# Turning quantised weights behind a mixture of experts, and a gather that is added part by part

## The chip, the cores and the metric

The kernel runs as one program on one core of a Trainium2 chip. The metric is the device time of the whole program in microseconds (us); less is better. Five engines work side by side: TensorE (PE, matmuls and transposes), VectorE (DVE), ScalarE (ACT), GpSimd (POOL, which here also issues the indirect DMAs) and SyncE (SP, which issues the plain DMAs). Each engine runs its own list of instructions in the order in which the program was written, and waits on semaphores that the others raise.

## The reference, cut to what matters

Two decoder layers work on x of shape 32 x 256 x 256 (32 items of 256 tokens of 256 features). The change lies at the seam between the experts that end the first layer and the attention that begins the second.

```
# end of layer 0: one expert for each token, 16 experts of 512 places, hidden size 1024
h = relu(einsum('ecd,edh->ech', buf, W1) + b1);  y = einsum('ech,ehd->ecd', h, W2) + b2
x = x + where(keep, y[idx, safe_pos] * gate, 0)
# start of layer 1: attention over the 32 items of each token position
n = layernorm(x);  q = n @ Wq.T;  k = n @ Wk.T
x = x + softmax(tanh(scores(q, k) / 16), over items) @ n
...
# end of layer 1: a gated feed-forward whose three matrices (w_gate, w_up: 704x256, w_down: 256x704)
# are quantised to FP4 in blocks of 16 along the last dimension; the matmuls need them transposed
gate = xq @ q(w_gate).T;  up = xq @ q(w_up).T;  out = hq @ q(w_down).T
```

## The kernel before, in words

The program is four phases written one behind the other, each closed by an all-engine barrier: phase A (rotary and cross attention of layer 0 with the router), phase C (the experts), phase D (the attention over the items), phase E (cross attention of layer 1 and the quantised feed-forward). Queues within a phase are written out by hand: phase C as a loop over the experts, phases D and E by tables of slots, where `due(n, period, slots, items)` says which step of which item stands at place n of an engine's list.

**Phase C.** For each of 16 experts e, `pe_phase_c` writes on PE: eight up groups (`pe_c_up`, 2 matmuls of 512 columns each into banks 0 to 3), the transposes of the next expert's tokens (`pe_c_turn`, banks 6 and 7), for e = 4 to 14 one step of `pe_weights` (the transposes of a piece of a quantised matrix, 11 steps in all, `TURNS`), and four down groups (`pe_c_down`, 8 matmuls each, banks 4 and 5). `pe_weights` uses bank 6 or 7, and so waits for ACT to have copied the next expert's tokens out of that bank (`act_c_x_t`); `act_weights` then copies the piece into `ff_wg`, `ff_wu` or `ff_wd`, which are read in phase E only. The quantising itself (`dve_weights`, 30 steps on DVE) stands beside experts 1 to 4. `sp_c_out` stores each expert's answer into the DRAM tensor `expert_out`; behind the last one SP waits until all stores have landed (`y_out`), and then the barrier of line 1853 follows.

**Phase D.** 16 steps t, each of G = 4 parts g of 128 rows. POOL gathers the rows of `expert_out` that belong to the step's tokens (`pool_d_gather`, four indirect DMAs, one for each part, into `sa_y`). DVE waits for all four, multiplies by the gate and adds x (`dve_d_add`, four instructions), makes the layer norm's moments (`dve_d_moments`: four BN_STATS, four aggregates, one addition); POOL raises the variance to -1/2 (`pool_d_power`); DVE normalises (`dve_d_normed`); PE transposes (`pe_d_turn`), projects (`pe_d_project`), makes the scores (`pe_d_score`) and, after tanh, exp and a mask, the sums (`pe_d_sum`). DVE adds the sums to x (`dve_d_out`), SP stores them and then loads the x, slots and gates of four steps on. x, slots and gates of steps 0 to 3 are loaded during phase C.

The order of POOL's list in phase D is that of the table: gather at place 2 + 2t, power at place 5 + 2t. So the gather of step 1 (place 4) stands ahead of the power of step 0 (place 5), the gather of step 2 (place 6) behind it. `pool_d_gather` waits for the step's x, slots and gates, and for the add of step t - 2, whose `sa_y` buffer it takes.

Of the kernel before, what the change touches and what calls it, by code (L numbers as in the profile page):

```python
# [11 lines left out]
ALU = mybir.AluOpType  # L12
# [11 lines left out]
KC = D // P  # L24
# [39 lines left out]
class Core:  # L64
# [13 lines left out]
        self.steps = {self.pool_made.name: 0, self.dve_made.name: 0, self.pe_made.name: 0}  # L78
        self.end_phase()

    def end_phase(self):
        self.idle_sems += reversed(self.phase_sems)
        self.phase_sems = []

        self.bank_out = [(self.idle, 0)] * 8

        self.p_out = [(self.idle, 0)] * 8

# [36 lines left out]
    return t - lag if 0 <= t - lag < n else None  # L125


def due(n, period, slots, items=B):

    for k, slot in enumerate(slots):  # L130
        b, off = divmod(n - slot, period)
        if off == 0 and 0 <= b < items:
            yield b, k


# [1360 lines left out]

FC = -(-FI // P)  # L1500
WIDTHS = [min(P, FI - k * P) for k in range(FC)]
HALF = FI // 2
# [283 lines left out]
def pe_phase_c(c):  # L1786
    for k in range(KC):
        pe_c_turn(c, 0, k)
    for e in range(E):
        for m1 in range(MC):  # L1790
            pe_c_up(c, e, m1)
        if e + 1 < E:
            for k in range(KC):
                pe_c_turn(c, e + 1, k)
        if e == 3:
            pe_positions(c)
        if 4 <= e < 4 + TURNS:
            pe_weights(c, e - 4)
        for q in range(QC):
            pe_c_down(c, e, q)  # L1800


def act_phase_c(c):
    for k in range(KC):
        act_c_x_t(c, 0, k)
    for e in range(E):
        for m1 in range(0, MC, 2):
            act_c_hidden(c, e, m1)
        if e + 1 < E:
            for k in range(KC):  # L1810
                act_c_x_t(c, e + 1, k)
        if e == 3:
            act_positions(c)
        if 4 <= e < 4 + TURNS:
            act_weights(c, e - 4)


def dve_phase_c(c):
# [27 lines left out]
def phase_c(c, d):  # L1846
    setup_c(c)
    raw_weights(c)
    sp_phase_c(c, d)
    pe_phase_c(c)  # L1850
    act_phase_c(c)
    dve_phase_c(c)
    c.nc.all_engine_barrier()  # L1853

# [51 lines left out]
def setup_d(c):  # L1908
    nc, r, s = c.nc, c.sa, c.sa.s
    r.y, r.x3 = c.ring("sa_y", 2, [P, G, D]), c.ring("sa_x3", 4, [P, G, D])  # L1910
    r.out, r.xn = c.ring("sa_out", 2, [P, G, D]), c.ring("sa_xn", 4, [P, G, D + 1])
    r.xn_t, r.q = c.ring("sa_xnt", 2, [P, KC, G * P]), c.ring("sa_q", 2, [P, KC, G * P])
    r.weight, r.rec = c.ring("sa_p", 2, [P, G, P]), c.sb("sa_rec", [P, G])
    r.stats, r.mv = c.sb("sa_stats", [P, G, 6]), c.sb("sa_mv", [P, G, 2])
    r.var, r.rstd = c.sb("sa_var", [P, G]), c.sb("sa_rstd", [P, G])
    n = STEPS_D
    s.y_in = [c.new_sem(f"sa_y_in{i}") for i in range(2)]
    s.x3, s.ln, s.pow = c.sem("sa_x3", n), c.sem("sa_ln", 4 * n), c.sem("sa_pow", n)
    s.turned, s.xn_t = c.sem("sa_xnT", 2 * n), c.sem("sa_xnt", 2 * n)
    s.projected, s.q = c.sem("sa_proj", 2 * n), c.sem("sa_q", 2 * n)  # L1920
    s.scored, s.tanh, s.exp, s.weight = (c.sem("sa_" + name, n) for name in ("score", "tanh", "exp", "w"))
    s.summed, s.rec, s.out, s.out_there = c.sem("sa_pv", 4 * n), c.sem("sa_rec", 4 * n), c.sem("sa_done", 4 * n), c.pair("sa_out_there", 16 * n // 2)
    for ring in range(4):
        c.step(c.dve_made, nc.vector.memset(r.xn[ring][:, :, D:D + 1], 1.0))
    c.dve.wait_ge(*c.all_of(c.dve_made))
    c.dve.wait_ge(s.same, 1)
    c.pe.wait_ge(s.both, 1)
# [25 lines left out]
def pool_d_gather(c, answer, t):  # L1953
    s, r, par = c.sa.s, c.sa, t % 2
    c.pool.wait_ge(s.x_in[t % 4], 48 * (t // 4 + 1))
    c.pool.wait_ge(s.x3, t - 1)
    for g in range(G):
        c.nc.gpsimd.indirect_dma_start(  # L1958
            r.y[par][:, g, :], None, answer, bass.IndirectOffsetOnAxis(ap=r.slot[t % 4][:, g:g + 1], axis=0),
            bounds_check=answer.shape[0] - 1, oob_is_err=False).then_inc(s.y_in[par], 16)  # L1960


def dve_d_add(c, t):

    s, r, dve, par, at = c.sa.s, c.sa, c.nc.vector, t % 2, t % 4
    c.dve.wait_ge(s.x_in[at], 48 * (t // 4 + 1))
    c.dve.wait_ge(s.y_in[par], 64 * (t // 2 + 1))
    c.dve.wait_ge(s.out, 4 * (t - 3))
    for g in range(G):
        m = dve.scalar_tensor_tensor(out=r.x3[at][:, g, :], in0=r.y[par][:, g, :], scalar=r.gate[at][:, g:g + 1],  # L1970
                                     in1=r.x[at][:, g, :], op0=ALU.mult, op1=ALU.add)
    m.then_inc(s.x3, 1)


def dve_d_moments(c, t):
    s, r, dve, at = c.sa.s, c.sa, c.nc.vector, t % 4
    c.dve.wait_ge(s.x3, t + 1)
    for g in range(G):
        m = dve.bn_stats(r.stats[:, g, :], r.x3[at][:, g, :])
    m.then_inc(s.ln, 1)  # L1980
# [624 lines left out]
def build(nc, d):  # L2605
# [5 lines left out]
    with ExitStack() as ctx:  # L2611
# [5 lines left out]
        for phase in (phase_a, phase_c, phase_d, phase_e):  # L2617
# [51 lines left out]
```

## Time and profile before

| | us |
|---|---|
| median of three runs | 3308.53 |
| the runs | 3308.53, 3306.96, 3313.92 |
| profiled execution, device time | 3310.97 |
| profiled execution, span from the first to the last instruction | 3309.2 |
| of it PE busy | 3089.0 (93%) |
| DVE busy | 2335.3 (71%) |
| ACT busy | 1786.9 (54%) |
| POOL busy | 1278.0 (39%) |
| mean granted TensorE clock | 0.971 |

All times within the trace are us from the span's start. The phases' borders in it: phase A to about 1380, phase C to about 1856, phase D to about 2025, phase E to the end. Of the 1.8 us between the span and the device time of the same execution nothing is in the trace. A row of the timeline gives start, duration, engine, line, operation, the tiles written and read, how many instructions it merges (x), and in brackets how long the engine sat idle before it and what ended that. Matmul ends are modelled, so a following row may begin a little before the one above it ends.

### The profile page before, as it was taken

What the parts mean: (1) busy time and instruction counts of PE and PEld (TensorE: products, weight loads), DVE (VectorE), ACT (ScalarE), POOL (GpSimd) and SP (SyncE); (2) the same over time, 40 slices, a digit from 0 to 9 for tenths busy, and PEclk for the clock granted to TensorE, in tenths of its full rate; (3) what the DMA queues carried; (4) which work ended last, traced back from release to release, by engine and by line L of the source; (5) the groups of instructions that cost most, each with busy time, mean ns of one, the idle gap of its engine ahead of it and who ended that gap; (6) DMA issues with size and microseconds to landing.
All of it is one profiled execution on the core that took longest, in us unless ns stands there. A gap on an engine that the chain in (4) does not pass through costs nothing. (4 is left out here: it accounts for less than half of the span.)

```text
span 3309.2 us, 57683 instructions
## 1 busy us (share of the span) xinstructions
PE 3089.0 (93%) x21302; PEld 2142.9 (65%) x21302; DVE 2335.3 (71%) x4796; ACT 1786.9 (54%) x3245; POOL 1278.0 (39%) x1929
## 2 busy tenths in 40 slices
PE   3799999999999998699999796899999999999998
PEld 2566666666666665366666454567777777777765
DVE  4588888888888887242111385587788877888786
ACT  3788888888888874211111132455555555555553
POOL 4366666666666663100000361133333333333321
PEclk8999999999999998799999897899999999999999
DMA  5887788887788882333234253433344333433330
GB/s 108 140 129 102 110 111 111 114 114 102 106 110 111 111 102 44 124 119 114 96 109 145 64 172 94 72 57 57 62 72 64 59 57 62 71 63 61 57 49 14
DMA packets 291117, 301.17 MB, mean 91 GB/s; under 512 B 35258, under 2 KB 278442, under 8 KB 290836
## 3 DMA queue, kind: packets, MB, share of 16 engines
q1 hardware_dynamic: 276436, 273.41, 48.9%
q0 software_dynamic: 6144, 15.68, 1.9%
q10 hardware_dynamic: 8256, 8.39, 0.8%
q8 instruction: 169, 2.77, 0.4%
q14 instruction: 112, 0.92, 0.1%
HBM read 95.51 MB, written 50.40 MB: 44 GB/s over the span
## 5 line engine op out<-in xcount | busy, mean ns | idle before, releaser
L493 DVE TENSOR_REDUCE xa_mx<-bank 128x2 f32<-128x512 f32 x1024 | 664.2, 687 | 257.8 <-PE bank L483 251.0
L597 ACT ACTIVATE xa_p<-bank 128x512 f32<-128x512 f32 x1024 | 566.3, 598 | 294.0 <-PE bank L587 270.9
L608 DVE SCALAR_TENSOR_TENSOR xa_p<-xa_p,bank 128x1024 f32<-128x1024 f32 x256 | 303.6, 1217 | 30.0 <-ACT xa_p L597 22.9
L620 PE MATMUL bank<-xa_p,xa_v 128*32 128x256 f32 x4096 | 278.6, 390 | 0.5 <-DVE xa_p L608 0.3
L1958 POOL DMA_INDIRECT sa_y<-expert_out,sa_s x64 | 70.6, 1103 | 522.6 <-POOLq L1853 483.4
L933 POOL TENSOR_SCALAR_AFFINE_SELECT xa_p<-xa_p 128x256 f32<-128x256 f32 x512 | 197.0, 407 | 174.9 <-ACT xa_p L924 174.7
L924 ACT ACTIVATE xa_p<-bank 128x384 f32<-128x384 f32 x512 | 231.0, 495 | 51.3 <-PE bank L912 39.9
L1747 ACT ACTIVATE ex_h<-bank,ex_b 128x512 f32<-128x512 f32 x64 | 44.0, 687 | 362.4 <-PE bank L1736 362.4
L1736 PE MATMUL bank<-ex_xt,ex_w 128*128 128x512 f32 x512 | 225.2, 598 | 0.7 <-ACT ex_xt L1727 0.7
L1766 PE MATMUL bank<-ex_w,ex_h 128*128 128x256 f32 x1024 | 224.0, 379 | 1.0 <-issue 0.9
L1766 PEld LDWEIGHTS bank<-ex_w,ex_h 128*128 128x128 f32 x1024 | 193.4, 190 | 28.1 <-issue 2.4
L587 PE MATMUL bank<-xa_qs,xa_ks 99*128 99x256 bf16 x1024 | 185.5, 277 | 13.9 <-DMA xa_qs<-xa_row 5.3
L483 PE MATMUL bank<-xa_ks,xa_qs 96*128 96x256 bf16 x1024 | 187.4, 277 | 8.4 <-DVE xa_mx L493 5.9
L2294 ACT ACTIVATE fe_g<-bank 128x352 f32<-128x352 f32 x128 | 59.1, 462 | 241.3 <-PE bank L2276 240.8
L483 PE MATMUL bank<-xa_ks,ex_w 96*128 96x256 bf16 x1024 | 174.3, 277 | 15.5 <-DMA ex_w<-xa_pq 10.4
L1551 POOL TENSOR_TENSOR fp_v<-fp_v,fp_p 128x1408 f32<-128x1408 f32 x31 | 98.5, 3179 | 230.2 <-DVE fp_v L1542 230.2
L587 PE MATMUL bank<-ex_w,xa_ks 99*128 99x256 bf16 x1024 | 170.3, 277 | 10.5 <-DMA ex_w<-xa_row 7.8
L454 PE MATMUL bank<-ff_wd,fe_ht 128*128 128x256 f32 x744 | 168.9, 383 | 7.4 <-ACT fe_ht L1651 6.1
L2276 PE MATMUL bank<-ff_wg,fe_xnt 128*128 128x352 f32 x512 | 172.8, 460 | 3.0 <-DVE ex_w L2310 1.6
L1736 PEld LDWEIGHTS bank<-ex_xt,ex_w 128*128 128x128 f32 x512 | 98.3, 192 | 118.3 <-issue 116.5
L1776 DVE TENSOR_TENSOR ex_y<-bank,ex_b 128x256 f32<-128x256 f32 x64 | 27.2, 425 | 203.6 <-PE bank L1766 203.6
L620 PEld LDWEIGHTS bank<-xa_p,xa_v 128*32 128x32 f32 x4096 | 107.9, 110 | 94.8 <-issue 49.4
(294 smaller groups left out, 6933.5 us busy)
## 6 DMA issues: line engine op xcount, KB each, us to landing
ex_w<-ra_parts SPq DMA_DIRECT2D x384, 128.0 KB, 7.0
xa_ks<-xa_pk SPq DMA_DIRECT2D x384, 128.0 KB, 5.4
ex_w<-in_L_ffn_W SPq DMA_DIRECT2D x32, 1024.0 KB, 7.1
xa_qs<-xa_pq SPq DMA_DIRECT2D x192, 128.0 KB, 4.7
ex_w<-xa_pq SPq DMA_DIRECT2D x192, 128.0 KB, 4.5
ra_x<-in_x SPq DMA_DIRECT2D x32, 256.0 KB
xa_ctx<-in_ctx_t SPq DMA_DIRECT2D x64, 128.0 KB
queue<-zeros ACTq DMA_DIRECT2D x4, 2048.0 KB, 14.0
```

Source lines behind the costliest of these rows:

```text
L454: m = c.nc.tensor.matmul(ps[:, tc * D:(tc + 1) * D], left[:, k, tc * P:(tc + 1) * P], right[:, k, :], start=(k == 0), stop=(k == chunks - 1))
L483: m = c.nc.tensor.matmul(ps[:, tc * S:(tc + 1) * S], c.xa.q_stack[par][0:STACK3, h, tc * P:(tc + 1) * P], c.xa.k_stack[par][0:STACK3, h, : ...
L493: c.nc.vector.tensor_reduce(c.xa.row_max[:, :, n], halves(c.banks[2 + n % 2]), AX.X, ALU.max).then_inc(s.max_taken, 1)
L587: m = c.nc.tensor.matmul(ps[:, kc * S:(kc + 1) * S], c.xa.k_stack[par][:, h, kc * P:(kc + 1) * P], c.xa.q_stack[par][:, h, :], start=True, ...
L597: c.nc.scalar.activation(c.xa.p_beside[:, n // 2 % 4, :, n % 2, :], halves(c.banks[n % 2]), ACT.Exp, scale=SCALE).then_inc(s.exp, 1)
L608: c.nc.vector.scalar_tensor_tensor(out=p, in0=p, scalar=1.0, in1=c.banks[bank][:, :].unsqueeze(1).broadcast_to([P, TC, 2 * S]), op0=ALU.mi ...
L620: m = c.nc.tensor.matmul(bank[WIDE * quad:WIDE * quad + WIDE, at + q0:at + S], v[:, kc, 4 * g + quad, :], p(4 * g + quad, kc), start=(kc = ...
L924: c.nc.scalar.activation(c.xa.p_after[:, n // 2 % 4, n % 2, 0:S + P], c.banks[n % 2][:, 0:S + P], ACT.Exp, scale=1.0 / math.sqrt(2.0 * DH) ...
L933: c.nc.gpsimd.affine_select(out=diagonal, in_=diagonal, compare_op=ALU.is_ge, fill=0.0, base=0, pattern=[[0, TC], [1, P]], channel_multipl ...
L1736: m = c.nc.tensor.matmul(c.banks[bank][:, :], r.w1[par][:, k, m1 * P:(m1 + 1) * P], r.x_t[par][:, k, :], start=(k == 0), stop=(k == KC - 1))
L1766: m = c.nc.tensor.matmul(c.banks[bank][:, 0:D], r.hid[par][:, k, q * P:(q + 1) * P], r.w2[par][:, k, :], start=(k == 0), stop=(k == MC - 1))
L2276: m = c.nc.tensor.matmul(c.banks[bank][:, 0:HALF], c.ff.xn_t[:, k, tc * P:(tc + 1) * P], w[:, k, cols], start=(k == 0), stop=(k == KC - 1))
```

## The change

1. The 11 steps of `pe_weights` and `act_weights` leave the loop over the experts and stand behind it, on PE and on ACT, one after the other.
2. The barrier between phases C and D is gone. In its place POOL waits for the stores of `expert_out`. SP's own wait for them stays. `end_phase` keeps what banks 6 and 7 wait for, so that phase D's first transposes wait for ACT's last copies; some tiles of phase D are declared in another order.
3. Step 0 of phase D gets a function of its own, `dve_d_first`: each of the four gathers raises its own semaphore, and DVE adds a part and takes its BN_STATS as soon as that part is there. Its aggregates follow.
4. On POOL the gather and the power of step 0 are written ahead of the table, which begins with step 1.

The parts of the diff that matter:

```diff
@@ pe_phase_c @@
-        if 4 <= e < 4 + TURNS:
-            pe_weights(c, e - 4)
         for q in range(QC):
             pe_c_down(c, e, q)
+    for n in range(TURNS):
+        pe_weights(c, n)
@@ act_phase_c @@
-        if 4 <= e < 4 + TURNS:
-            act_weights(c, e - 4)
+    for n in range(TURNS):
+        act_weights(c, n)
@@ phase_c @@
-    c.nc.all_engine_barrier()
+    for out in c.ex.s.y_out:
+        c.pool.wait_ge(out, 16 * (E // 2))
@@ pool_d_gather @@
-            bounds_check=answer.shape[0] - 1, oob_is_err=False).then_inc(s.y_in[par], 16)
+            bounds_check=answer.shape[0] - 1, oob_is_err=False).then_inc(s.y_in[par] if t else s.y_first[g], 16)
@@ new @@
+def dve_d_first(c):
+    s, r, dve = c.sa.s, c.sa, c.nc.vector
+    c.dve.wait_ge(s.x_in[0], 48)
+    for g in range(G):
+        c.dve.wait_ge(s.y_first[g], 16)
+        m = dve.scalar_tensor_tensor(out=r.x3[0][:, g, :], in0=r.y[0][:, g, :], scalar=r.gate[0][:, g:g + 1],
+                                     in1=r.x[0][:, g, :], op0=ALU.mult, op1=ALU.add)
+        done = (s.x3_first, g + 1) if g < G - 1 else (s.x3, 1)
+        m.then_inc(done[0], 1)
+        c.dve.wait_ge(*done)
+        m = dve.bn_stats(r.stats[:, g, :], r.x3[0][:, g, :])
+    m.then_inc(s.ln, 1)
+    dve_d_moments(c, 0)
@@ dve_phase_d @@
+    dve_d_first(c)
...
-        for b, _ in due(n, period, (16,), STEPS_D):
+        for b, _ in due(n, period, (16,), STEPS_D, first=1):
@@ pool_phase_d @@
+    pool_d_gather(c, d["expert_out"], 0)
+    pool_d_power(c, 0)
...
-        for b, _ in due(n, period, (2,), STEPS_D):
+        for b, _ in due(n, period, (2,), STEPS_D, first=1):
             pool_d_gather(c, d["expert_out"], b)
-        for b, _ in due(n, period, (5,), STEPS_D):
+        for b, _ in due(n, period, (5,), STEPS_D, first=1):
             pool_d_power(c, b)
```

TensorE's list before, from the last expert with a weight step to phase D's first transposes (`raw_down` is the quantised w_down, `ex_x` an expert's tokens, `ex_h` its hidden values, `sa_xn` phase D's normalised rows):

```order
L1736 MATMUL bank<-ex_xt,ex_w 128x512 x16
L1718 MATMUL bank<-ident,ex_x 128x128 x8
L304 MATMUL bank<-ident,raw_down 128x128 x2
L304 MATMUL bank<-ident,raw_down 64x128 x2
L1766 MATMUL bank<-ex_w,ex_h 128x256 x32
L1736 MATMUL bank<-ex_xt,ex_w 128x512 x16
L1766 MATMUL bank<-ex_w,ex_h 128x256 x32
L2011 MATMUL bank<-ident,sa_xn 128x128 x8
```

And the same place now (lines are those of the changed file):

```order
L1738 MATMUL bank<-ex_xt,ex_w 128x512 x16
L1720 MATMUL bank<-ident,ex_x 128x128 x8
L1768 MATMUL bank<-ex_w,ex_h 128x256 x32
L1738 MATMUL bank<-ex_xt,ex_w 128x512 x16
L1768 MATMUL bank<-ex_w,ex_h 128x256 x32
L1626 MATMUL bank<-ident,raw_gate 128x128 x12
L1626 MATMUL bank<-ident,raw_up 128x128 x12
L306 MATMUL bank<-ident,raw_down 128x128 x10
L306 MATMUL bank<-ident,raw_down 64x128 x2
L2033 MATMUL bank<-ident,sa_xn 128x128 x8
```

All 36 transposes of matrices now stand in one row between the last expert's down matmuls and phase D's first transposes.

POOL's list before, at the start of phase D (the number behind `sa_y` is the buffer, that behind `sa_s` the ring place of the step's slots, 0 to 3 for steps 0 to 3):

```order
L1958 DMA sa_y0<-expert_out,sa_s0 128x256 x4
L1958 DMA sa_y1<-expert_out,sa_s1 128x256 x4
L1993 TENSOR_TENSOR sa_rstd<-sa_var,mhalf 128x4
L1958 DMA sa_y0<-expert_out,sa_s2 128x256 x4
L1993 TENSOR_TENSOR sa_rstd<-sa_var,mhalf 128x4
```

And now:

```order
L1963 DMA sa_y0<-expert_out,sa_s0 128x256 x4
L2015 TENSOR_TENSOR sa_rstd<-sa_var,mhalf 128x4
L1963 DMA sa_y1<-expert_out,sa_s1 128x256 x4
L1963 DMA sa_y0<-expert_out,sa_s2 128x256 x4
L2015 TENSOR_TENSOR sa_rstd<-sa_var,mhalf 128x4
```

The gather of step 1 has moved from ahead of the power of step 0 to behind it, and stands together with the gather of step 2. From the power of step 1 on the two lists are alike.

## Rows read from the trace of the kernel before

**Rows 1.** Windows by phase, C and D: busy us, (x instructions), clock, DMA, GB/s

```profile
core 0: us, PE busy (x) PEld busy (x) DVE busy (x) ACT busy (x) POOL busy (x), PEclk, DMA share, GB/s
...
1380.00:1856.00 476.00, 468.47 (x1710) 312.36 (x1710) 106.80 (x157) 67.87 (x110) 0.00 (x0) 0.99 0.35 115
1856.00:2025.30 169.30, 138.20 (x641) 88.67 (x640) 125.89 (x419) 54.50 (x96) 87.16 (x80) 0.93 0.43 137
```

**Rows 2.** Timeline of PE in phase C: start, duration, what

```profile
1414.24 13.90 PE L1736 MATMUL bank<-ex_xt,ex_w 128*128 128x512 f32 x32
...
1442.92 13.90 PE L1736 MATMUL bank<-ex_xt,ex_w 128*128 128x512 f32 x32
...
1502.81 13.90 PE L1736 MATMUL bank<-ex_xt,ex_w 128*128 128x512 f32 x32
1516.54 1.04 PE L1718 MATMUL bank<-ident,ex_x 128*128 128x128 f32 x8
1517.92 0.63 PE L1624 MATMUL bank<-ident,raw_gate 128*128 128x128 f32 x4 [0.34 <-ACT ex_xt L1727]
...
1827.18 13.90 PE L1736 MATMUL bank<-ex_xt,ex_w 128*128 128x512 f32 x32
```

**Rows 3.** ACT's copies of turned weights (line 1638): ns min/median/max

```profile
L1638 ACT ACTIVATE ff_wg<-bank x4: 330/464/597, 1518.6 to 1607.1; 128x512 f32<-128x512 f32 x2, 128x192 f32<-128x192 f32 x2
```

**Rows 4.** The barrier (line 1853) on SP's queue: ns, and start in us

```profile
L1853 SPq DRAIN  x1: 7/7/7, 1859.5 to 1859.5; - x1
...
L1853 SPq EVENT_SEMAPHORE  x1: 17/17/17, 1859.7 to 1859.7; - x1
```

**Rows 5.** Timeline of POOL at the start of phase D

```profile
1860.54 1.06 POOL L1958 DMA_INDIRECT sa_y<-expert_out,sa_s  x1 [483.43 <-POOLq L1853]
...
1864.52 1.00 POOL L1958 DMA_INDIRECT sa_y<-expert_out,sa_s  x1 [0.31 <-issue]
1865.82 1.00 POOL L1958 DMA_INDIRECT sa_y<-expert_out,sa_s  x1 [0.30 <-issue]
...
1869.88 0.99 POOL L1958 DMA_INDIRECT sa_y<-expert_out,sa_s  x1 [0.30 <-issue]
1871.25 1.04 POOL L1993 TENSOR_TENSOR sa_rstd<-sa_var,mhalf 128x4 f32<-128x4 f32 x1 [0.37 <-DVE sa_mv L1983]
1872.48 1.20 POOL L1958 DMA_INDIRECT sa_y<-expert_out,sa_s  x1 [0.19 <-issue]
...
1876.74 1.01 POOL L1958 DMA_INDIRECT sa_y<-expert_out,sa_s  x1 [0.30 <-issue]
```

**Rows 6.** Timeline of DVE at the start of phase D

```profile
1867.43 1.67 DVE L1970 SCALAR_TENSOR_TENSOR sa_x<-sa_y,sa_g,sa_x 128x256 f32<-128x256 f32 x4 [7.44 <-DMA sa_y<-expert_out,sa_s]
1869.13 1.41 DVE L1979 BATCH_NORM_STATS2 sa_stats<-sa_x 128x6 f32<-128x256 f32 x4
...
1872.33 1.44 DVE L2001 TENSOR_SCALAR sa_xn<-sa_x,sa_mv,sa_rstd 128x256 f32<-128x256 f32 x4 [1.17 <-POOL sa_rstd L1993]
1874.27 1.67 DVE L1970 SCALAR_TENSOR_TENSOR sa_x<-sa_y,sa_g,sa_x 128x256 f32<-128x256 f32 x4 [0.50 <-DMA sa_y<-expert_out,sa_s]
...
1879.17 1.44 DVE L2001 TENSOR_SCALAR sa_xn<-sa_x,sa_mv,sa_rstd 128x256 f32<-128x256 f32 x4 [1.16 <-POOL sa_rstd L1993]
```

**Rows 7.** Timeline of PE in phase D: steps 0 and 1, and the transposes of step 15

```profile
1873.82 1.97 PE L2011 MATMUL bank<-ident,sa_xn 128*128 128x128 f32 x8 [17.80 <-DVE sa_xn L2001]
...
1882.48 2.05 PE L2048 MATMUL bank<-sa_q,sa_xnt 128*128 128x128 f32 x16 [0.69 <-ACT sa_q L2039]
1884.37 1.04 PE L2011 MATMUL bank<-ident,sa_xn 128*128 128x128 f32 x8
...
2011.05 1.09 PE L2011 MATMUL bank<-ident,sa_xn 128*128 128x128 f32 x8 [0.22 <-DVE sa_xn L2001]
```

**Rows 8.** Window of the 6 us behind PE's restart (columns as in Rows 1)

```profile
1873.80:1879.80 6.00, 5.29 (x12) 3.07 (x13) 4.26 (x15) 1.19 (x2) 4.67 (x5) 0.50 0.32 90
```

**Rows 9.** Waits in phase D, one group: us in total, times, longest us

```profile
POOL sa_y L1958 <- DMA sa_g<-gates: 23.7, 11, 3.2
```

**Rows 10.** Timeline of POOL in phase D, the longest of the 64 gather instructions

```profile
1950.76 1.90 POOL L1958 DMA_INDIRECT sa_y<-expert_out,sa_s  x1 [0.30 <-issue]
```

More of the change, by code:

```diff
@@ L79, in __init__, with end_phase @@
         self.end_phase()
-    def end_phase(self):
+    def end_phase(self, banks=()):
         self.idle_sems += reversed(self.phase_sems)
         self.phase_sems = []
-        self.bank_out = [(self.idle, 0)] * 8
+        self.bank_out = [self.bank_out[i] if i in banks else (self.idle, 0) for i in range(8)]
         self.p_out = [(self.idle, 0)] * 8
@@ L125, in item, with due @@
     return t - lag if 0 <= t - lag < n else None
-def due(n, period, slots, items=B):
+def due(n, period, slots, items=B, first=0):
     for k, slot in enumerate(slots):
         b, off = divmod(n - slot, period)
-        if off == 0 and 0 <= b < items:
+        if off == 0 and first <= b < items:
             yield b, k
@@ L1579, in raw_weights @@
     s.loaded, s.quant = c.sem("weights_in", 16 * 11), c.sem("weights_fp4", 30)
-    s.turned, s.copied = c.sem("weightsT", TURNS), c.sem("weights_t", TURNS)
+    s.turned, s.copied = c.sem("weightsT"), c.sem("weights_t")
     for raw in f.raw[0:2]:
@@ L1910, in setup_d @@
     r.y, r.x3 = c.ring("sa_y", 2, [P, G, D]), c.ring("sa_x3", 4, [P, G, D])
[L1911 to L1914, printed above, removed]
+    r.xn, r.xn_t = c.ring("sa_xn", 4, [P, G, D + 1]), c.ring("sa_xnt", 2, [P, KC, G * P])
+    r.stats, r.mv, r.rec = c.sb("sa_stats", [P, G, 6]), c.sb("sa_mv", [P, G, 2]), c.sb("sa_rec", [P, G])
     r.var, r.rstd = c.sb("sa_var", [P, G]), c.sb("sa_rstd", [P, G])
+    r.q, r.out, r.weight = c.ring("sa_q", 2, [P, KC, G * P]), c.ring("sa_out", 2, [P, G, D]), c.ring("sa_p", 2, [P, G, P])
     n = STEPS_D
-    s.y_in = [c.new_sem(f"sa_y_in{i}") for i in range(2)]
+    s.y_in, s.y_first = [c.new_sem(f"sa_y_in{i}") for i in range(2)], [c.new_sem(f"sa_y_first{g}") for g in range(G)]
+    s.x3_first = c.sem("sa_x3_first")
     s.x3, s.ln, s.pow = c.sem("sa_x3", n), c.sem("sa_ln", 4 * n), c.sem("sa_pow", n)
@@ L1966, in dve_d_add @@
     c.dve.wait_ge(s.x_in[at], 48 * (t // 4 + 1))
-    c.dve.wait_ge(s.y_in[par], 64 * (t // 2 + 1))
+    c.dve.wait_ge(s.y_in[par], 64 * (t // 2 + par))
     c.dve.wait_ge(s.out, 4 * (t - 3))
@@ L1972, in dve_d_add @@
     m.then_inc(s.x3, 1)
+def dve_d_first(c):
[11 more added lines that the diff above has]
+    dve_d_moments(c, 0)
 def dve_d_moments(c, t):
     s, r, dve, at = c.sa.s, c.sa, c.nc.vector, t % 4
[L1977 to L1980, printed above, removed]
+    if t:
+        c.dve.wait_ge(s.x3, t + 1)
+        for g in range(G):
+            m = dve.bn_stats(r.stats[:, g, :], r.x3[at][:, g, :])
+        m.then_inc(s.ln, 1)
     c.dve.wait_ge(s.ln, 4 * t + 1)
@@ L2120, in dve_phase_d @@
 def dve_phase_d(c):
+    dve_d_first(c)
     period = ROUND_D["dve"]
     for n in range((STEPS_D - 1) * period + 40):
-        for b, _ in due(n, period, (16,), STEPS_D):
+        for b, _ in due(n, period, (16,), STEPS_D, first=1):
             dve_d_add(c, b)
-        for b, _ in due(n, period, (18,), STEPS_D):
+        for b, _ in due(n, period, (18,), STEPS_D, first=1):
             dve_d_moments(c, b)
@@ L2623, in build @@
                 phase(c, d)
-            c.end_phase()
+            c.end_phase((6, 7) if phase is phase_c else ())
 def kernel(**inputs):
```

## The prediction

> **What bounds the kernel now.** First the windows by phase [rows 1]. In phase C PE is busy 468.5 of 476 us, at full clock: the experts are bound by PE, DVE and ACT are mostly idle and POOL does nothing. So there a microsecond that leaves PE's path is a microsecond of the kernel. Phase D (169.3 us) has PE at 138.2 and DVE at 125.9, and its start is a hole: PE's last down matmul ends at 1856.0, its next work begins at 1873.82 after 17.8 us idle [rows 7]. That hole is a chain: store of the last expert, barrier, four gathers, add, moments, power, normalise, transposes. Next I read PE's timeline in phase C for what a round (one expert) takes with and without a weight step, then POOL, DVE and PE at the seam in that order, since the chain goes from one to the next. Phase E stands behind a barrier of its own and is not touched; it moves as a block.
>
> **Turns leave the rounds.** A round without a turn takes 1442.92 - 1414.24 = 28.68 us [rows 2]. That round has quantising steps on DVE beside it and is no slower for it. The eleven rounds with a turn run from 1502.81 to 1827.18, 324.37 us [rows 2], or 29.49 each. Eleven plain rounds would take 11 x 28.68 = 315.48. The difference is **8.9 us**. Its make-up is seen in the first of them: the token transposes start at 1516.54 and the turn only at 1517.92 after a wait of 0.34 us for ACT's copy of those tokens out of the bank, so one pays for a bank wait as well as for the transposes. All of it lies on PE's path, with the hidden values ready: nothing else is late in the plain rounds. I see no reason for the removed turns to leave less than this; what bounds it is that rounds of both kinds are equal to 0.3 us among themselves, so 8.5 to 9.1.
>
> **Turns behind the rounds.** They now run on PE and ACT after the last down matmul. PE's four transposes take 0.63 us [rows 2], ACT's copy 0.33 or 0.60 [rows 3]. Two banks alternate; one bank needs transposes, copy and two hand-overs of some 0.2 to 0.3 us, about 1.6 us for a pair of steps on both banks, so eleven steps take about 5.5 x 1.6 = 9 us, and 11 x (0.63 + 0.60 + 0.5) = 19 us were nothing to overlap. The cover is the hole: 17.8 us before, some 15.3 after the next two terms. I take 0; without any overlap it would be late by 4. For the last expert nothing is queued behind the turns that the chain needs: its answers are added on DVE and stored by SP.
>
> **Barrier.** SP sees the stores landed at 1859.5 and the barrier lets go at 1859.7 [rows 4]; the first gather starts at 1860.54 [rows 5]. POOL now waits for the same stores itself. The 0.2 us go for sure; the 0.84 us between release and gather may be set-up that stays. Bounds 0 to 1.0, I take **0.3**, nearest to the barrier's own rows.
>
> **First residual.** The last of four gathers starts at 1864.52, DVE is released at 1867.43: 2.91 us to landing. The gathers start 1.3 us apart, and one part's add (1.67/4 = 0.42) and statistics (1.41/4 = 0.35) [rows 6] fit between two of them. So behind the last landing stand one add and one statistic (some 0.9 with the extra hand-over) in place of 1.67 + 1.41 = 3.08: **2.2 us** less. With the barrier's 0.3 the power of step 0 moves from 1871.25 to 1868.75 and PE's first transposes from 1873.82 to 1871.3.
>
> [...] What the trace shows: a gather instruction takes 1.0 us, and 1.90 at its longest [rows 10]. [...]
>
> **Where that gain goes.** It reaches the rest only if step 1 comes earlier too, and here the order on POOL counts. Before, step 1's gathers ran at 1865.82 to 1870.9, ahead of power 0, while POOL waited for DVE anyway [rows 5]. Now they stand behind power 0. From the power's start to the first gather behind it are 1872.48 - 1871.25 = 1.23 us, so step 1's first gather starts at 1868.75 + 1.23 = 1869.98, **4.2 us later** than before. The last of the four starts 1876.74 - 1872.48 = 4.26 later, at 1874.24. To landing: 2.91 (step 0), or 1874.27 - 1869.88 = 4.39 (step 1) [rows 5, 6]. The slower one had step 4's load issued right beside it; that load is released by the first add, and so now comes well ahead. I take 2.91: add 1 at 1877.15 (before 1874.27). Then as before: 4.90 us from add to normalise, and 1.49 to the transposes [rows 6, 7]: PE's step 1 at 1883.54, against **1884.37** before, where it only queued behind step 0's scores (1882.48 + 2.05). Those scores now end at 1882.0, so PE idles 1.5 us. Of a head start of 2.5 us **0.8** is left. With the slower landing step 1 comes at 1885.0, 0.7 later than before.
>
> From here the two kernels have the same lists, and PE runs back to back. The gather of step 2 stands ahead of power 1 in both. It would end at about 1880.7, and power 1 is wanted at 1877.15 + 3.82 = 1881.0: just clear. The low clock changes nothing: before, the clock was 0.50 until 6 us after PE's restart [rows 8]. I assume the same again at 1871.3. Were it full, the first transposes and projections would be done earlier, but the transposes of step 1 wait for DVE all the same.
>
> **The sum.** -8.9 (rounds) - 0.8 (what is left at step 1) = **-9.7 us**. The profiled span becomes 3309.2 - 9.7 = 3299.5. That execution took 3310.97, 2.4 above the median of 3308.53; against the median I predict **3298.8 us**. Own range of this case: rounds 8.5 to 9.1, step 1 from -1.9 (barrier 1.0 instead of 0.3, landing half a us quicker) to +0.7, so 3297.5 to 3300.7.
>
> **Rivals.**
> - The head start holds: step 1 is ready when PE is, and 2.5 us reach the end. -8.9 - 2.5: **3297.1**. Against: it needs add 1 at 1875.6, 5.6 us after its first gather, where the two rows show 6.9 and 8.4. Chance 0.10.
> - Late gathers: a slow landing (4.39), or DVE's part-wise adds holding two gathers for 0.42 each, or power 1 held by gather 2. Step 1 comes at 1885 to 1886, phase D starts 0.7 to 1.5 us later than before. -8.9 + 1: **3300.6**. [...] For it: the margin at power 1 is 0.3 us, and gathers up to 1.90 exist. Chance 0.25.
> - The rounds don't get shorter, since something else fills the turn's place (the tokens' copies, the weights' loads). -0.8 alone: **3307.7**, no change. Against: three plain rounds at 28.7. Half of the gain would be 3303. Chance 0.05.
> - Slower: phase D's steady loop slips. Step 1 to step 15 take 2011.05 - 1884.37 = 126.7 us, 9.05 each [rows 7], and POOL waits in 11 steps for the gates' load, 23.7 us in all [rows 9], with the power of the step before queued behind that gather. If the shifted start left the load of every step about 0.7 us later against its gather, the power would be late by as much each time: 14 x 0.7 = 9.8, just the gain. From 0.7 us a step on the kernel is slower; at 1.2, 3308.5 - 9.7 + 16.8 = **3315.6**. Against: the load follows the step's own output, so loop and load shift together. Chance 0.03.
>
> **How the numbers follow.** Forecast 0.57, the rivals 0.10, 0.25, 0.05, 0.03. Median to median, a measurement of this kernel can tell about 0.2% (6.6 us) from no change; the three runs alone spread from 3306.96 to 3313.92. Faster by over 0.2% means below 3301.9: forecast, head start, and nearly all of the late gathers, 0.91. Within 0.2%: 0.06. Slower: 0.03. The range takes in the head start, the late gathers, and some 1.5 us for the medians: 3295.5 to 3302.5.
>
> **What would show it.** Rounds 4 to 14 of phase C at 28.7 us each. 36 transposes of matrices behind the last down matmul, done before phase D's first transposes. Four adds in four separate places on DVE, with only one behind the last landing. Step 1's gathers behind power 0, and PE idle for about 1.5 us ahead of its transposes, whose distance from the last expert's down matmuls (1856.0 to 1884.37, 28.4 us) falls by only 0.8. The prediction is wrong if this distance falls by 2 or more (head start), if it grows, or if the rounds keep more than 0.3 us of the turns.

## The result and the profile after

| | before | changed kernel |
|---|---|---|
| median | 3310.22 us (10 runs) | 3302.21 us (10 runs) |
| spread of the runs | 3304.76 to 3313.92 | 3297.49 to 3306.20 |
| profiled execution, device time | 3310.97 us | 3298.72 us |
| its span | 3309.2 us | 3297.0 us |
| its mean granted TensorE clock | 0.971 | 0.979 |

The ratio of the two is 0.9978, with a 95% interval of 0.9969 to 0.9986: 7.3 us less (4.6 to 10.3); the two medians lie 8.0 apart. The change makes the kernel faster, by somewhat less than the 9.7 us forecast. The two profiled executions differ by more than the medians, 12.2 us (3310.97 to 3298.72), and the first thing to see is where. The timeline of PE in the changed kernel (start, duration, what; `ex_h` hidden values, `raw_...` the quantised matrices, `sa_xn` phase D's normalised rows):

```profile
1379.47 1.97 PE L1720 MATMUL bank<-ident,ex_x 128*128 128x128 f32 x8 [12.79 <-DMA ex_x<-queue]
1382.12 15.66 PE L1738 MATMUL bank<-ex_xt,ex_w 128*128 128x512 f32 x32 [0.69 <-ACT ex_xt L1729]
...
1412.61 13.90 PE L1738 MATMUL bank<-ex_xt,ex_w 128*128 128x512 f32 x32
...
1501.18 13.90 PE L1738 MATMUL bank<-ex_xt,ex_w 128*128 128x512 f32 x32
...
1816.61 13.90 PE L1738 MATMUL bank<-ex_xt,ex_w 128*128 128x512 f32 x32
1831.40 14.05 PE L1768 MATMUL bank<-ex_w,ex_h 128*128 128x256 f32 x64 [0.89 <-issue]
1845.29 0.82 PE L1626 MATMUL bank<-ident,raw_gate 128*128 128x128 f32 x6
...
1852.07 0.66 PE L306 MATMUL bank<-ident,raw_down 128*128 128x128 f32 x4 [0.25 <-ACT ff_wd L1650]
1860.79 1.97 PE L2033 MATMUL bank<-ident,sa_xn 128*128 128x128 f32 x8 [8.07 <-DVE sa_xn L2023]
1863.45 5.34 PE L2051 MATMUL bank<-sa_xnt,sa_wqk 128*128 128x512 f32 x8 [0.69 <-ACT sa_xnt L2043]
1869.48 2.05 PE L2070 MATMUL bank<-sa_q,sa_xnt 128*128 128x128 f32 x16 [0.69 <-ACT sa_q L2061]
1873.18 1.09 PE L2033 MATMUL bank<-ident,sa_xn 128*128 128x128 f32 x8 [1.65 <-DVE sa_xn L2023]
```

These rows answer to [rows 2, 7]. The eleven rounds run from 1501.18 to 1816.61, 315.43 us for 324.37: **8.94** less. From the last down matmul's end (1831.40 + 14.05 = 1845.45) to step 1's transposes (1873.18) are 27.73 us for 28.35: **0.62** less. Together 9.56. The other 2.6 us lie where nothing was changed: phase C begins 0.5 earlier, its first round (1382.12 to 1412.61, 30.49 for 31.59 us) is 1.1 shorter, since the granted clock rose earlier (1.00 from 1385.5 on, where before it was still 0.50 at 1387.5), and what follows step 1, phase E with it, is 1.0 shorter.

Here are POOL and DVE at the seam, the place where phase C ends and phase D begins; they answer to [rows 5, 6]. First POOL:

```profile
1849.75 1.06 POOL L1963 DMA_INDIRECT sa_y<-expert_out,sa_s  x1 [474.05 <-DMA expert_out<-ex_y]
...
1853.73 1.00 POOL L1963 DMA_INDIRECT sa_y<-expert_out,sa_s  x1 [0.31 <-issue]
1858.22 1.04 POOL L2015 TENSOR_TENSOR sa_rstd<-sa_var,mhalf 128x4 f32<-128x4 f32 x1 [3.49 <-DVE sa_var L2009]
1859.45 1.20 POOL L1963 DMA_INDIRECT sa_y<-expert_out,sa_s  x1 [0.19 <-issue]
...
1863.59 1.01 POOL L1963 DMA_INDIRECT sa_y<-expert_out,sa_s  x1 [0.30 <-issue]
```

Then DVE:

```profile
1852.71 0.48 DVE L1986 SCALAR_TENSOR_TENSOR sa_x<-sa_y,sa_g,sa_x 128x256 f32<-128x256 f32 x1 [6.75 <-DMA sa_y<-expert_out,sa_s]
...
1856.57 0.48 DVE L1986 SCALAR_TENSOR_TENSOR sa_x<-sa_y,sa_g,sa_x 128x256 f32<-128x256 f32 x1 [0.35 <-DMA sa_y<-expert_out,sa_s]
1857.09 0.43 DVE L1991 BATCH_NORM_STATS2 sa_stats<-sa_x 128x6 f32<-128x256 f32 x1
...
1866.78 1.67 DVE L1975 SCALAR_TENSOR_TENSOR sa_x<-sa_y,sa_g,sa_x 128x256 f32<-128x256 f32 x4 [6.04 <-DMA sa_y<-expert_out,sa_s]
```

POOL's first gather is now let go by the store's landing itself, not by the barrier. The part-wise adds wait for one landing each, and one add stands behind the last. POOL idles 3.49 us ahead of power 0, and step 1's first gather comes at 1859.45 only, 9.70 us behind step 0's first; before, it was 5.28 (1860.54 to 1865.82). DVE then waits 6.04 us for step 1's rows, and PE 1.65 us for DVE. So the fourth of the changes (POOL's new order) takes back most of what the third (the part-wise add) gives.

### The profile page after: what moved, and what is told of

It reads as the page before. It is cut to its first block and busy times, and to the rows that moved or that the text cites. A ratio compares the mean times of both kernels' runs of the same rounds, so it can differ in the third digit from the quotient of the medians.

```text
span 3297.0 us, 57673 instructions
## 1 busy us (share of the span) xinstructions
PE 3088.8 (94%) x21302; PEld 2141.7 (65%) x21302; DVE 2334.7 (71%) x4796; ACT 1786.0 (54%) x3245; POOL 1277.9 (39%) x1929
## 5 line engine op out<-in xcount | busy, mean ns | idle before, releaser
L610 DVE SCALAR_TENSOR_TENSOR xa_p<-xa_p,bank 128x1024 f32<-128x1024 f32 x256 | 303.4, 1215 | 30.2 <-ACT xa_p L599 23.2
L485 PE MATMUL bank<-xa_ks,ex_w 96*128 96x256 bf16 x1024 | 173.9, 276 | 15.8 <-DMA ex_w<-xa_pq 12.1
L2301 PE MATMUL bank<-ff_wu,fe_xnt 128*128 128x352 f32 x512 | 167.2, 459 | 0.6 <-ACT fe_g L2319 0.6
```

The source lines that it names most:

```text
L485: m = c.nc.tensor.matmul(ps[:, tc * S:(tc + 1) * S], c.xa.q_stack[par][0:STACK3, h, tc * P:(tc + 1) * P], c.xa.k_stack[par][0:STACK3, h, : ...
L610: c.nc.vector.scalar_tensor_tensor(out=p, in0=p, scalar=1.0, in1=c.banks[bank][:, :].unsqueeze(1).broadcast_to([P, TC, 2 * S]), op0=ALU.mi ...
L2301: m = c.nc.tensor.matmul(c.banks[bank][:, 0:HALF], c.ff.xn_t[:, k, tc * P:(tc + 1) * P], w[:, k, cols], start=(k == 0), stop=(k == KC - 1))
```

## The experiments

One measure serves for all: where things stand in the trace, counted from the end of the last expert's down matmuls. Two traces of the changed kernel agree in it to 0.3 us in the sum, two of the split gather to 0.1 (though two of its terms moved by 0.6 and 0.7, against each other), while the times of whole runs scatter by several us. Everything in a row of the table but the ratio comes from one trace of that kernel; the ratio rests on 5 to 11 runs of it. In the table "rounds" is the time of the eleven rounds of experts 4 to 14, "step 0" and "step 1" are the starts of phase D's first and second transposes, "to 15" the way from step 1's to step 15's transposes, and "path" the sum of the three differences to before (rounds, step 1, to 15). "By ratio" is the ratio to the kernel before, measured beside it, with its 95% interval.

| kernel | rounds | step 0 | step 1 | to 15 | path | by ratio |
|---|---|---|---|---|---|---|
| before | 324.37 | 17.80 | 28.35 | 126.68 | 0 | |
| changed kernel | 315.43 | 15.34 | 27.73 | 126.14 | -10.1 | 0.9978 (0.9969 to 0.9986) |
| after_again | 315.43 | 15.33 | 27.77 | 126.45 | -9.8 | 0.9974 (0.9965 to 0.9983) |
| turns_only | 315.43 | 22.28 | 33.49 | 126.87 | -3.6 | 0.9979 (0.9970 to 0.9988) |
| seam_only | 324.38 | 15.34 | 27.79 | 126.81 | -0.4 | 1.0 (0.999 to 1.001) |
| whole_first | 315.43 | 17.61 | 28.85 | 126.68 | -8.4 | 0.9977 (0.9968 to 0.9986) |
| old_pool_order | 315.43 | 17.14 | 28.38 | 126.34 | -9.3 | 0.9964 (0.9950 to 0.9978) |
| split_gather | 315.43 | 15.32 | 25.84 | 126.89 | -11.2 | 0.9967 (0.9955 to 0.9980) |
| split_again | 315.43 | 15.37 | 26.43 | 126.22 | -11.3 | 0.9965 (0.9951 to 0.9979) |
| warm_only | 315.43 | 22.57 | 30.63 | 127.19 | -6.2 | 0.9986 (0.9977 to 0.9996) |
| split_warm | 315.44 | 22.57 | 30.62 | 126.63 | -6.7 | 0.9980 (0.9970 to 0.9989) |
| warm9_only | 315.44 | 16.10 | 28.25 | 129.04 | -6.7 | 0.9978 (0.9968 to 0.9989) |
| warm9_split | 315.43 | 15.70 | 25.13 | 129.72 | -9.1 | 0.9961 (0.9947 to 0.9974) |
| turns_twice | 315.43 | 15.29 | 27.36 | 129.38 | -7.2 | 0.9973 (0.9962 to 0.9984) |

**The changed kernel again.**

> The changed kernel once more, nothing left out. Question: is the gain 9.6 us (path theory: 8.9 from the eleven rounds, 0.6 from the seam, as the two traces show them) or some 7 to 8 us, as the medians of the runs so far have it (3310.22 and 3302.21)? Path theory: the distance from the last expert's last down matmul to the transposes of step 1 of phase D is 27.7 us again, a round of the experts 28.68, and the medians differ by 9.6, give or take the 2 us by which medians of a kernel wander. Rival (something is given back later, in phase E): the gain stays under 8.0 and phase E is longer than before by 1.5 us or more in this trace too (it was 0.9 longer in the first).

Median 3302.65 us (11 runs) beside 3311.86 (33 runs of before): 9.2 between the medians, 8.6 by the ratio. Taken together, the means of the changed kernel's 21 runs and of the 43 runs of before beside them (3302.3 and 3310.9) lie 8.6 us apart, with a 95% interval of about 7.0 to 10.3, worked out from the scatter of these runs. Rounds and seam are the same to 0.05 us. The rival asked for a longer phase E; from its first matmuls to the end it took 1273.6 us here, 1277.4 in the changed kernel's first trace and 1276.5 in that of before. So no loss of phase E's is tied to the change; phase E wanders by 4 us with the same code in it.

**The turns alone.** The loop edits of the diff (`pe_phase_c`, `act_phase_c`) in the kernel before, nothing else:

> The kernel before with one edit: the eleven weight steps stand behind the loop over the experts on PE and on ACT; the barrier and phase D stay as they were. Path theory: rounds of 28.68 us, 8.9 less in the sum; but the barrier makes PE and ACT drain, and the last copy of weights ends 8.0 us behind the last down matmul (1853.4 against 1845.45 in the changed kernel), while the stores landed after 3.5. So the barrier opens some 4.3 us later than its stores would allow, and of 8.9 only 4.6 are left: median about 3305.6 beside 3310.2. Rival (the barrier costs the turns nothing, since the drain overlaps): the full 8.9, 3301.3.

The barrier on each queue of this kernel (ns, start in us), POOL's first gather behind it, and ACT's last copy of weights:

```profile
L1853 SPq DRAIN  x1: 7/7/7, 1853.0 to 1853.0; - x1
...
L1853 ACTq DRAIN  x1: 672/672/672, 1856.8 to 1856.8; - x1
L1853 SPq EVENT_SEMAPHORE  x1: 17/17/17, 1857.7 to 1857.7; - x1
...
1858.51 1.06 POOL L1958 DMA_INDIRECT sa_y<-expert_out,sa_s  x1 [479.27 <-POOLq L1853]
...
1857.10 0.36 ACT L1651 ACTIVATE ff_wd<-bank 64x256 f32<-64x256 f32 x1
```

SP is ready at 1853.0, the barrier opens at 1857.7, when ACT's last copy is done. The first transposes come 22.28 us behind the last down matmul for 17.80, 4.5 later (4.3 expected), step 1's 5.1 later. So of 8.9 us the barrier takes back 4.5, and a longer low clock in step 0 (projections of 5.99 us for 5.32) another 0.7. In the times this is not as clear: the ratio says 7.0 us (4.0 to 9.9). That interval leaves out the path's 3.6 by a little, and it holds the expected 4.6 as well as the rival's 8.9, and the 8.6 of the changed kernel's second set. The trace shows the mechanism, a first gather held until ACT's last copy; how much of it the whole time feels is not settled by the times.

**The seam alone.** The changed kernel with the weight steps back in the loop over the experts, on PE and on ACT; `end_phase` keeps bank 6 only:

> The changed kernel with the eleven weight steps put back into the rounds of experts 4 to 14, on PE and ACT; the missing barrier, the part-wise first add and POOL's new order stay. Path theory: rounds of 29.5 us as before, first transposes of phase D 2.5 us earlier against the last down matmul than before (15.3 for 17.8 us), transposes of step 1 only 0.6 earlier (27.7 for 28.35): total 0.6 less than before, 3309.6 beside 3310.2, which the times can't tell from no change. Rival (the seam carries more of the gain than its first step shows): 2 us or more less, with step 1 at 26 us or under.

Ratio 1.0 (0.999 to 1.001), step 1 at 27.79. The first transposes come 2.5 us earlier, and nothing of it arrives at step 1 but 0.6. Step 0's projections took 5.95 us here for 5.34 in the changed kernel, and step 1 stands at the same place: PE still idled 1.11 us ahead of it, for DVE. The medians (3308.88 beside 3311.86) lie 3 apart, inside their scatter.

**Without the part-wise add.** The third and fourth change are undone: step 0's gathers raise the table's semaphore again, DVE waits for all four, and POOL has its old order. The parts of the edit that matter:

```diff
-    dve_d_first(c)
...
-    pool_d_gather(c, d["expert_out"], 0)
-    pool_d_power(c, 0)
...
-        for b, _ in due(n, period, (2,), STEPS_D, first=1):
+        for b, _ in due(n, period, (2,), STEPS_D):
```

> The changed kernel without its third and fourth edit: step 0 of phase D waits for all four gathers again and adds them in one go, and POOL has its old order (gather of step 1 ahead of power 0). Turns behind the rounds and no barrier. Path theory: the first transposes come 2.2 us later than in the changed kernel (17.5 us behind the last down matmul for 15.3), but step 1 is ready when PE is, so its transposes stand at 28.1 for 27.7: total only 0.4 more than the changed kernel. Rival (the part-wise add is worth its 2.2 us): 2.2 more than the changed kernel.

Step 0 at 17.61, 2.3 later, and step 1 at 28.85, 1.1 later than the changed kernel where 0.4 was expected. The 0.7 more is PE's clock: step 0's projections took 6.00 us here, 5.34 in the changed kernel. In time it can't be told from the changed kernel (0.9977 and 0.9978). So the third and the fourth change together bring step 1 forward by 1.1 us, 0.7 of it the clock's, and no run shows them in the time.

**POOL's order.** With `pool_d_gather(c, d["expert_out"], 1)` between the gather and the power of step 0, and the table's gathers from step 2 on:

> The changed kernel with one edit: on POOL the four gathers of step 1 stand ahead of power 0 again, as before the change; the part-wise add stays. Order theory: the gathers run while POOL waits for DVE (3.5 us idle) but end 1.7 us behind the moment at which power 0 could start, so the first transposes come about 1.7 later than in the changed kernel (17.0 us behind the last down matmul for 15.3); step 1's add comes some 4 us earlier, and step 1's transposes wait for PE instead of for DVE: 27.5 for 27.7 us. Total the same within 0.2 us. Rival (step 1's gathers were not what held its transposes): step 1's transposes stay behind the first by as much as now, 12.4 us, and come at 29.4.

Step 0 at 17.14 as expected; step 1 at 28.38, not 27.5, again because the projections took 6.01 us at the low clock. The rival (step 1 at 29.4) falls: with the gathers early, step 1's transposes follow step 0's scores without idling. So POOL's order only chooses which of the two waits. Its five runs gave 0.9964, with an interval wide enough to hold the path's 9.3. That ratio is no worse than the split gather's below, though the paths differ by 1.9 us: the times of so few runs don't rank these orders, the traces do.

**Two gathers ahead, two behind.**

```diff
     pool_d_gather(c, d["expert_out"], 0)
+    pool_d_gather(c, d["expert_out"], 1, range(0, 2))
     pool_d_power(c, 0)
+    pool_d_gather(c, d["expert_out"], 1, range(2, G))
...
-        for b, _ in due(n, period, (2,), STEPS_D, first=1):
+        for b, _ in due(n, period, (2,), STEPS_D, first=2):
```

> The changed kernel with one edit: two of the four gathers of step 1 stand ahead of power 0, two behind it. Order theory: two gathers (2.6 us) fit into POOL's 3.5 us of waiting, so power 0 and the first transposes stay where they are (15.3 us behind the last down matmul), the last gather of step 1 lands 2.6 us earlier, and step 1's transposes come when PE is free, 25.9 to 26.0 us for 27.7: 1.8 us less than the changed kernel, and the head start of 2.4 is kept whole against before. Rival (landing slows as gathers come together with step 4's load, or power 0 is pushed): 27 us or more.

POOL's timeline in this kernel, then PE's:

```profile
1857.22 1.00 POOL L1963 DMA_INDIRECT sa_y<-expert_out,sa_s  x1 [0.30 <-issue]
1859.08 1.05 POOL L2015 TENSOR_TENSOR sa_rstd<-sa_var,mhalf 128x4 f32<-128x4 f32 x1 [0.86 <-DVE sa_var L2009]
...
1861.66 1.97 PE L2033 MATMUL bank<-ident,sa_xn 128*128 128x128 f32 x8 [8.04 <-DVE sa_xn L2023]
1864.32 5.29 PE L2051 MATMUL bank<-sa_xnt,sa_wqk 128*128 128x512 f32 x8 [0.69 <-ACT sa_xnt L2043]
1870.29 2.05 PE L2070 MATMUL bank<-sa_q,sa_xnt 128*128 128x128 f32 x16 [0.69 <-ACT sa_q L2061]
1872.18 1.04 PE L2033 MATMUL bank<-ident,sa_xn 128*128 128x128 f32 x8
```

POOL's wait ahead of power 0 shrinks from 3.49 to 0.86 us, power 0 is not pushed, and PE no longer waits for step 1: 25.84 us, 2.5 less than before. This is the whole head start. It was run once more:

> The split gather once more, nothing left out, to see whether it beats both kernels by more than single traces tell. Path theory: 8.9 from the rounds, 2.5 from the seam (step 1's transposes at 25.8 us behind the last down matmul for 28.35 before), so 11.4 less than before, a ratio of 0.9965; a round of 28.68. Rival (the seam's gain is lost again in phase D, as the kernel with 9 unused matmuls lost 3 us there): the way from step 1's to step 15's transposes is 128 us or more for 126.7, and the ratio is 0.9973 as of the changed kernel.

3301.04 us beside 3311.81, ratio 0.9965; step 1 at 26.43, 0.6 above the first time and above the 25.8 expected, and 126.22 us from there to step 15. The 0.6 is the low clock again: step 0's projections took 5.83 us for 5.29, and here PE is what step 1 waits for. Both ratios (0.9967, 0.9965) lie below both of the changed kernel (0.9978, 0.9974), though the intervals overlap. Of all kernels here this one has the longest path gain: 11.2 and 11.3 us for 9.8 to 10.1.

**PE kept busy over the hole.**

```diff
 def pe_phase_d(c):
+    for _ in range(18):
+        c.nc.tensor.matmul(c.banks[0][:, :], c.consts.ident[:, :], c.sa.both[:, :, :], start=True, stop=True)
```

> The changed kernel with 18 matmuls of 512 columns added on PE ahead of phase D, their result not used (computation unchanged otherwise); they fill PE's idle 8 us between the last turned weight and the first transposes. Theory: the granted clock stays at 1.0, so the first transposes take 1.04 for 1.97 us and the first projection 3.70 for 5.34, step 0's scores end 2.5 us earlier; step 1's transposes wait for DVE and stay at 27.7 us, so the total is the same within 0.3 us. Rival (the low clock lies on the path): step 1's transposes come earlier too, by 1 us or more.

> Both edits together: two of step 1's gathers ahead of power 0, and the 18 unused matmuls that fill PE's idle time. Theory: with the split gather step 1's transposes wait for PE, whose first projection ran at the low clock; with the clock at 1.0 they wait for DVE again, at about 25.1 us behind the last down matmul: 0.9 less than the split gather alone, 2.6 less than the changed kernel, so that the clock counts only once the gathers do not hold. Rival: no more than the split gather alone, 25.9.

Both were mis-sized: one such matmul is two rows of 0.43 us in the trace, so 18 last 15.6 us and themselves put step 0 at 22.57, against an expected 15.3; on the path they lost some 4 us against the same kernels without them, and neither answers its rival. They show one thing cleanly: with the granted clock at 1.00, step 1 follows step 0 by 8.06 us, where PE is what binds it (10.5 to 11.2 at the low clock). With 9:

> As the warm_only kernel, with 9 unused matmuls for 18: there each took 0.87 us (two passes of 0.43), so that 18 lasted 15.6 us and pushed the first transposes to 22.6 us; 9 last 7.8 and end ahead of the first transposes. Theory: clock 1.0 throughout, first transposes at 15.3 to 15.5 us behind the last down matmul, step 0's scores done 2.5 us earlier, step 1's transposes where DVE lets them: 27.7 us as in the changed kernel. Rival (the low clock lies on the path of the changed kernel): step 1 at 26.7 or less.

> The split gather (two of step 1's gathers ahead of power 0, two behind) with the 9 unused matmuls. Theory: the clock stays at 1.0 and step 1's transposes wait for DVE again, at about 25.1 us behind the last down matmul, for 25.84 with the split gather alone and 27.73 in the changed kernel; total 2.6 less than the changed kernel. Rival (the split gather's step 1 was held by DVE or the landing, not by PE's low clock): 25.8 again.

PE's timeline in the kernel with 9 unused matmuls and the changed kernel's gathers:

```profile
1867.14 1.09 PE L2033 MATMUL bank<-ident,sa_xn 128*128 128x128 f32 x8 [1.09 <-DVE sa_xn L2023]
1868.97 3.70 PE L2051 MATMUL bank<-sa_xnt,sa_wqk 128*128 128x512 f32 x8 [0.74 <-issue]
1873.36 2.05 PE L2070 MATMUL bank<-sa_q,sa_xnt 128*128 128x128 f32 x16 [0.69 <-ACT sa_q L2061]
1879.29 1.97 PE L2033 MATMUL bank<-ident,sa_xn 128*128 128x128 f32 x8 [3.88 <-DVE sa_xn L2023]
1881.94 5.58 PE L2051 MATMUL bank<-sa_xnt,sa_wqk 128*128 128x512 f32 x8 [0.69 <-ACT sa_xnt L2043]
```

Step 0 runs at full clock (1.09 and 3.70) and starts at 16.10 for the 15.3 to 15.5 expected, since its last gather landed later (3.56 us from its start to the add, 2.84 in the changed kernel); step 1 waits for DVE, as expected, at 28.25 for 27.7. But now PE has 3.88 us of nothing in front of step 1, and the low clock comes there instead. The windows of this kernel (columns as in [rows 1]; the clock is the third number from the end):

```profile
1877.00:1878.00 1.00, 0.00 (x0) 0.00 (x0) 0.21 (x1) 0.00 (x0) 0.81 (x2) 1.00 0.47 131
...
1879.00:1880.00 1.00, 0.71 (x4) 0.72 (x5) 1.00 (x4) 0.00 (x0) 0.69 (x2) 0.50 0.19 37
```

The transposes take 1.97, the projections 5.58, and step 15 comes 129.04 us behind step 1 for 126.1 to 127.2 in all the others but warm9_split and turns_twice, which follow. On the path the low clock's cost was not removed, it was moved to step 1. The time doesn't show the loss: 0.9978, as for the changed kernel. With the split gather step 1 comes at 25.13, as expected, and the clock stays full through its first steps; that trace then lost 3.0 us later, between steps 4 and 6 (10.74 and 9.77 us for two steps of about 9.1) and between steps 7 and 8 (10.48). POOL in it, ahead of step 5:

```profile
1903.70 1.07 POOL L1963 DMA_INDIRECT sa_y<-expert_out,sa_s  x1 [3.60 <-DMA sa_g<-gates]
1905.08 1.83 POOL L1963 DMA_INDIRECT sa_y<-expert_out,sa_s  x1 [0.31 <-issue]
...
1909.57 1.04 POOL L2015 TENSOR_TENSOR sa_rstd<-sa_var,mhalf 128x4 f32<-128x4 f32 x1
```

The gather waited 3.60 us for the gates, one instruction took 1.83 us, and the power stood behind them: the loop of the fourth rival, in single steps. PE idled 2.04 us for it, and the low clock came back for a part of step 5 (0.50 from 1914 to 1916, projections of 4.84 us for 3.70). The trace of warm_only has one such step too, from step 13 to 14 (10.47 us, with a wait of 4.04 us for the gates on POOL); no trace without unused matmuls has one. Whether that is chance is open. The five runs of warm9_split gave the lowest ratio of all, 0.9961, and its interval (8.6 to 17.6 us) holds the trace's 9.1 only at its end, and has the 12.1 that the path would give without the lost steps near its middle: this speaks against a loss in every run.

**The turns twice.** Every weight step behind the rounds made two times:

> The changed kernel with every weight step behind the rounds made twice (22 steps for 11, the same results written again). It measures the cover. Theory: eleven steps took 8.0 us, so 22 end at 15.9 us behind the last down matmul, 0.6 later than the first transposes could start (15.3): these come at 15.5 to 16.2; step 1's transposes wait for DVE and stay at 27.7, so doubling the hidden work costs nothing, and PE's clock stays at 1.0 or falls only after the restart. Rival (the turns are not free: they slow the gathers, the copies or the last answers): step 1 at 28.5 or later, total up by 1 us or more.

Step 0 at 15.29, step 1 at 27.36: the seam doesn't feel eleven more turns, so the cover is real and not used up. Here too PE stayed busy up to step 0, ran it at full clock, and then idled 3.80 us ahead of step 1, and the low clock (0.50; step 1's transposes 1.48 us for 1.09, its projections 6.27 for 3.70) cost 2.7 us behind it (129.38). The expectation had "costs nothing", and its rival had the total up by 1 us or more; step 1 is not later, but the path as a whole is up: 2.9 us more than in the changed kernel. The turns themselves hold nothing up at step 0 or step 1; the loss is the clock's, but the added turns brought it, by moving PE's gap. The time (0.9973) shows no loss beside the changed kernel's 0.9978.

## Why the prediction came out as it did

**Rounds.** 8.9 forecast, 8.94 in every trace of a kernel with the edit. Right.

**Turns behind the rounds.** Some 9 us forecast, 8.0 measured, inside the hole: PE's down matmuls end at 1845.45 and ACT's last copy ends at 1853.41. The hand-overs, estimated at 0.2 to 0.3 us each, lie in this trace within the idle times between one piece and the next, 0.25 to 0.56 us on PE and 0.26 to 0.59 on ACT.

```profile
1853.05 0.36 ACT L1653 ACTIVATE ff_wd<-bank 64x256 f32<-64x256 f32 x1
```

Right; doubling them left step 0 where it was.

**Barrier.** 0.3 forecast: from the last down matmul to the first gather 4.30 us for 4.52, so 0.22. The prediction priced it by its own few tenths. What it would have cost with the turns behind it, 4.5 us at step 0, is missing from the prediction: the second edit is what makes the first one free, and as a part of the sum it was undervalued.

**First residual.** 2.2 forecast: from the first gather to the first transposes 11.04 us for 13.28, 2.24. Right. The rival of late gathers also counted with two gathers held for 0.42 us each by the part-wise adds; no run shows that term. The gathers beside the adds took 1.00 us and started 1.3 apart as before, and the adds took 0.48 us each, beside a gather (1852.71, 1853.92) as well as behind the last one (1856.57).

**Where the gain goes.** 0.8 forecast to be left, 0.62 measured. The mechanism, POOL's order, is shown by the split gather, which gets 2.5. The term off was the landing: 3.19 us from the last gather's start (1863.59) to DVE's release (1866.78), taken as 2.91; the four gathers gave 0.12 of it back, starting within 4.14 us for 4.26.

**The low clock.** "Changes nothing" was right for the changed kernel, and for seam_only, since DVE binds step 1 there (PE idled 1.65 and 1.11 us ahead of it, for DVE). Where PE binds it, with no idle time of PE ahead of it, the end of the low clock decides. The granted clock rose from 0.50 to 1.00 about 5.9 us behind PE's restart in before and 7.3 us behind it in whole_first and old_pool_order, and that is 0.7 us of step 1 (11.24 for 10.55 us from step 0 to step 1). Before, then whole_first:

```profile
1879.00:1880.00 1.00, 1.00 (x3) 0.42 (x2) 0.83 (x3) 0.00 (x0) 0.81 (x2) 0.62 0.01 4
...
1869.30:1870.30 1.00, 1.00 (x3) 0.48 (x2) 1.00 (x4) 0.60 (x1) 0.70 (x2) 0.53 0.00 0
1870.30:1871.30 1.00, 1.00 (x3) 0.20 (x2) 0.96 (x3) 0.00 (x0) 0.70 (x2) 1.00 0.42 131
```

**The sum and the range.** Rounds and step 1 together gave 9.6 us in the first trace, with the way to step 15 9.8 to 10.1; the forecast was 9.7. The times gave 7.3 (4.6 to 10.3) and 8.6 (5.6 to 11.6): both intervals hold it. The step that failed is the last term of the range, "some 1.5 us for the medians", and with it the median of three runs, 3308.53, as the place to count from. Ten runs of the same kernel gave 3310.22, and later sets 3311.86, 3308.9, 3312.36 and 3311.81. The measured 3302.21 is 3.4 us above the 3298.8 predicted: 1.7 because the kernel before had its median that much higher, 1.7 because the medians lie 8.0 apart and not 9.7. In us 3302.21 is still just inside the range, but against the new median the range's upper end is a ratio of 3302.5 / 3310.22 = 0.9977, and the measured one is 0.9978. And 0.91 for a time below 3301.9 was too sure for a forecast with that scatter beside it. That the 1.7 us missing between the medians are scatter fits the 8.6 of both sets together (7.0 to 10.3); no trace shows what they consist of, and a small loss in every run is not ruled out. Where a scatter of this size sits can be read from the traces: with the same code in them phase C began between 1379.2 and 1385.3 us and phase E took 1273.4 to 1277.9. A range for a measured median should have taken 3 to 4 us for that, twice what I took; the terms of the sum needed no more.

**The rivals.** Head start held (0.10): no, though the split gather shows it could be had. Late gathers (0.25): step 1 came 0.2 later than forecast, no more. Rounds not shorter: no. The slipping loop: not in the changed kernel; single steps of it in warm9_split.

## What to carry to other kernels

A move off the busy engine's path can be priced by a round without it against a round with it, and a barrier must be priced with what is put in front of it, not with its own length. When the first step of a pipeline is made earlier, follow the second step through every queue: here one shared list (POOL's) decided whether 0.6 or 2.5 us arrived, and splitting the second step's work around the first step's gave both. Filling PE's idle time ahead of step 0 with unused matmuls held the granted clock at 1.00 there, but brought step 1 forward only in warm9_split, where 1.16 us of idle time were left ahead of step 1 (25.13 us for 25.84 and 26.43 with the split gather alone), and that trace lost 3.0 us between later steps. With 3.88 us left ahead of step 1 (warm9_only) step 1 came at 28.25 for 27.73, and the path's gain was 6.7 for 10.1.

## What the hardware showed that I had not expected

- In two traces a gap moved was a low clock moved: with PE busy up to step 0, a gap of 3.88 us ahead of step 1 was followed by transposes of 1.97 us and projections of 5.58 at a granted clock of 0.50 (warm9_only; 3.70 at 1.00), and step 15 came 2.4 us later; in turns_twice, behind a gap of 3.80 us (transposes of 1.48 us, projections of 6.27), it was 2.7. With a gap of 1.65 us at the same place (changed kernel) the projections of step 1 took 3.70.
- How long the low clock lasts behind a restart differs between executions by more than 1 us (5.9 to 7.3 at the start of phase D); the same restart at the start of phase C made its first round 30.2 to 31.9 us long.
- A matmul of 512 f32 columns stands as two rows of 0.43 us in the trace (x18 for 9 instructions).
